# A latent attention layer and a six-layer local transformer on one core: shifted rows by two whole-tile transposes and ten small transfers, weight preparations placed one by one, another order of the pieces

## The chip, the cores and the metric

One core of a Trainium2 chip runs the whole program. Its engines are TensorE (PE; its weight loads are listed apart as PEld), VectorE (DVE), ScalarE (ACT), GpSimd (POOL) and SyncE (SP, which here only starts transfers). Each runs its own list of instructions in order and waits on semaphores for the others. The metric is the device time of one launch in microseconds (us); lower is better.

## The reference

The input is 2 batches of 1024 positions of 128 channels, float32. It is normalised; then the sum of three things is returned: the input, a causal attention with 8 heads over latent keys and values, and a transformer of 6 layers with local attention. Cut to the part that the change touches:

```python
def shift_tokens(t):                     # the upper 64 channels come from the position before
    a, s = jnp.split(t, 2, -1)
    s = jnp.pad(s, ((0, 0), (1, 0), (0, 0)))[:, :-1]
    return jnp.concatenate([a, s], -1)
def attn_layer(x, Wqkv, qs, ksc, Wo):    # 16 heads of 64, windows of 32 that also see the window before
    q, k, v = split(x @ Wqkv)
    q, k = rotate(l2norm(q) * qs), rotate(l2norm(k) * ksc)
    return local_attention(q, k, v) @ Wo
def ffn_layer(x, g, bln, W1, b1, W2, b2):
    xn = (x - mean) / sqrt(var + 1e-05) * g + bln
    a, gate = split(xn @ W1 + b1)
    return a * gelu(gate) @ W2 + b2
for i in range(6):
    x = attn_layer(shift_tokens(x), ...) + x
    x = ffn_layer(shift_tokens(x), ...) + x
```

## The kernel before

The first fifth of the time is the latent attention, which the change leaves as it is. The rest is one loop, unrolled, over steps `G`. A tile is 128 positions; a layer has 16 tiles (8 of each batch) and six layers have 96. Step `G` does a piece of work for tile `G`, another for tile `G-1` and so on, so the stages of several tiles are in flight at once. Each engine's order is the order of the calls in its own `for G in range(STEPS)` block, written by hand; a call does nothing where its tile or chunk does not exist. `chunk_at(G, lag)` names a chunk of the feed-forward part (four tiles, 512 positions) in every fourth step.

What a tile goes through, with the PE function first: `project_keys` (matmuls from `xsH`, `xsL`, `qkH`, `qkL` into PSUM banks 0 and 1; ACT squares them, DVE multiplies by the cosine and sine tables, POOL adds and scales), `transpose_keys` (ACT `copy_keys`), the same for queries, `mask_scores` and `scores`, then maxima, subtraction, exponentials, denominators and scaling, `transpose_probs` (ACT `copy_probs`). `weigh_lower` and `weigh_upper` multiply the probabilities with the shifted input itself, since the value and output matrices have been multiplied into `M` beforehand (`products`, once a layer); ACT copies both halves (`copy_lower`, `copy_upper`), and `fold_lower` and `fold_upper` apply `M`. DVE adds the residual (`attended`), PE transposes for the layer norm (`ln_rows`, `ln_columns`). The feed-forward part is `up_gate` and `up_value` in three pieces `j` each, `down`, and DVE's `residual`, which writes the next layer's input `X`.

For the weighing, `weigh_*` needs each window of 32 positions together with the window before it, 64 rows in all, with positions on the partitions, twice (partitions 0 to 63 and 64 to 127), as `xw`. PE function `windows(k)` makes it straight from `X`: 4 windows, 2 copies and 2 halves of the channels, so 16 small matmuls with the identity into banks 4 and 5, and ACT's `copy_windows` moves the 128x512 result to `xw`.

Banks: 0 and 1 hold projections, 2 and 3 transposes and products, 4 and 5 scores and weighed sums, 6 and 7 the feed-forward pieces; 6 also the layer norm's columns, 7 the folded result. `claim(bank)` waits until its last contents have been read.

At the turn of a layer: ACT's `upper_weights` rounds the raw key and query weights (inside `square_keys` and `square_queries`) and POOL subtracts; PE's `products` runs twice after `fold_upper`, with ACT's `copy_products`; `shifts` makes the new bias terms with 12 passes of one column, DVE adds them (`biases`), and in the same DVE function waits for ACT's `upper_w1` to subtract the lower part of W1. SP loads the weights of the next layer in one run, as soon as each buffer is free; `W2` has one buffer.

Of the kernel before, what the change touches and what calls it, by code (L numbers as in the profile page):

```python
# [23 lines left out]
P = 128  # L24
B, T, D = 2, 1024, 128
NT = T // P
TILES = B * NT
# [30 lines left out]
STEPS = DEPTH * TILES + 12  # L58


RING = 2


M_BANK, XW, DN_BANK = 7, 4, 7
# [31 lines left out]
def build(nc, x, wqT, wkdT, wvd, wku, wvuT, wo, wqk, wvo, w1, w2, par, sca, cst_d, tab_d, out):  # L96
    ctx = ExitStack()
    with ctx:
# [21 lines left out]
        W2 = sb("W2", [P, 3, D])  # L120
# [32 lines left out]

        arena = sb("arena", [P, 17664])
# [6 lines left out]
        xw = arena[:, 11520:12032].rearrange("p (w c) -> p w c", w=NW)  # L161
# [47 lines left out]
        for n in ("k_mm q_mm kT_mm qT_mm s_mm pt_mm xw_mm z_mm o_mm lnT_mm lnB_mm g_mm0 g_mm1 g_mm2 a_mm0 a_mm1 a_mm2 f_mm M_mm b1_mm fin_mm "  # L209
                  "k_sq q_sq kT_cp qT_cp s_exp pt_cp xw_cp z_cp ln_cp xn_cp xn_H y_sq y_ln y_exp gl0 gl1 gl2 xs_H wk_H wq_H w1_H M_cp cst_cp "  # L210
# [4 lines left out]
        c_in, qk_in, wvo_in, w1_in, w2_in, sca_in, tab_in = (  # L215
            sem(n) for n in ("c_in", "qk_in", "wvo_in", "w1_in", "w2_in", "sca_in", "tab_in"))
# [77 lines left out]
        def _(sp):  # L294
# [25 lines left out]
            def load_w2(l):  # L320
                sp.dma_start(W2[:, :, :], w2[l]).then_inc(w2_in, 16)

# [6 lines left out]
            load_w2(0)  # L329
            load_par(0)  # L330
# [4 lines left out]
            for l in range(DEPTH):  # L335
                if l + 1 < DEPTH:

                    sp.wait_ge(s["tab"], 8 * l + 8)
                    load_scales(l + 1)
# [4 lines left out]
                    load_wvo(l + 1)  # L344
                    sp.wait_ge(s["w1_L"], l + 1)
                    sp.wait_ge(s["b1_mm"], l + 1)
                    load_w1(l + 1)

                    sp.wait_ge(s["f_mm"], NC * (l + 1))
                    load_w2(l + 1)  # L350
                    sp.wait_ge(s["x_new"], NC * (l + 1))
                    if l + 2 < DEPTH:
                        load_par(l + 2)
# [7 lines left out]
        def _(pool):  # L361
            credit(pool, "pool")
            pool.memset(X[:, :, 0:XO], 0.0).then_inc(s["zeroed"], 1)
            pool.memset(X1[:, :, 0:1], 0.0).then_inc(s["zeroed"], 1)
            pool.memset(xsH[:, :, 0:1].bitcast(F32), 0.0).then_inc(s["zeroed"], 1)
# [146 lines left out]
            for G in range(STEPS):  # L512
                lower_columns(G - 7)
                scale_queries(G - 2)
                next_key_weights(G - 1)
                rotate_keys(G - 1)
                scale_probs(G - 3)
                shifted_lower(chunk_at(G, 15))
                refine(G - 1)
# [990 lines left out]
```

## Time and profile before

| | us |
|---|---|
| median of 3 runs (2095.35 to 2100.75) | 2095.5 |
| the profiled execution's own time | 2100.06 |
| its span, first to last instruction | 2098.2 |
| PE busy | 1924.6 (92%) |
| DVE busy | 1560.9 (74%) |
| POOL busy | 1324.6 (63%) |
| ACT busy | 1290.3 (61%) |

Spans and positions below are in us from the start of the profiled execution; the loop of steps begins near 400. A busy share is that of one engine alone, so that several can be high at once. An engine's idle time matters only where nothing else would have kept the following work waiting.

### The profile page before, as it was taken

The numbers are of one execution on the slowest core, as the hardware profiler recorded it, in microseconds if no ns is written. First come the engines' busy times: TensorE is split into PE (matmuls) and PEld (weight loads), VectorE is DVE, ScalarE is ACT, GpSimd is POOL, SyncE is SP. The second block draws the span as 40 slices with busy tenths as digits, with TensorE's granted clock in tenths as the row PEclk, the third lists the DMA queues.
The fourth block names the chain that finished last, engine by engine and source line by source line (L and its number), as shares of the span: only waits on it lengthen the run. The fifth ranks groups of instructions, "written<-read, shape, count | busy, mean of one in ns | idle before, by whom it ended". The sixth has DMA issues, their size and how long they took to land. (4 is left out here: it accounts for less than half of the span.)

```text
span 2098.2 us, 65778 instructions
## 1 busy us (share of the span) xinstructions
PE 1924.6 (92%) x27244; PEld 1523.1 (73%) x27244; DVE 1560.9 (74%) x2684; ACT 1290.3 (61%) x2082; POOL 1324.6 (63%) x1145
## 2 busy tenths in 40 slices
PE   6888886699999999999999999999999999999996
PEld 4665665577777777777777777777777877787774
DVE  4766865777887778877777877788776878787773
ACT  5666765356566656665656666657665666566654
POOL 2332343677786667776667866588666777676760
PEclk9999998899999999999999999999998999999999
DMA  3000001000000010000010000100000100000000
GB/s 99 2 0 0 0 1 57 15 3 2 2 2 2 2 55 2 2 3 2 2 55 2 2 2 2 55 3 2 2 2 6 52 2 2 2 3 6 2 7 16
DMA packets 12434, 25.12 MB, mean 12 GB/s; under 512 B 1856, under 2 KB 9728, under 8 KB 10496
## 3 DMA queue, kind: packets, MB, share of 16 engines
q1 hardware_dynamic: 12160, 21.16, 2.9%
q8 instruction: 209, 3.42, 0.7%
q14 instruction: 65, 0.53, 0.1%
HBM read 20.11 MB, written 1.05 MB: 10 GB/s over the span
## 5 line engine op out<-in xcount | busy, mean ns | idle before, releaser
L1061 PE MATMUL banks<-arena 128*128 128x128 f32 (+4 forms) x6052 | 672.8, 311 | 60.0 <-ACT arena L689 16.8
L1061 PEld LDWEIGHTS banks<-arena 128*128 128x128 f32 (+3 forms) x6052 | 558.5, 176 | 169.8 <-issue 70.6
L902 DVE TENSOR_TENSOR arena<-banks,tabs 128x1024 f32<-128x1024 f32 x192 | 235.2, 1225 | 133.6 <-ACT arena L646 125.0
L449 POOL TENSOR_TENSOR arena<-arena 128x1024 f32<-128x1024 f32 x96 | 230.6, 2402 | 66.0 <-DVE arena L907 65.8
L479 POOL TENSOR_TENSOR small<-small 128x33 f32<-128x33 f32 x100 | 24.6, 246 | 350.2 <-ACT small L736 350.2
L675 ACT ACTIVATE arena<-banks 128x1024 f32<-128x1024 f32 x96 | 98.7, 1028 | 238.2 <-PE banks L1218 238.2
L444 POOL TENSOR_TENSOR prob<-prob,small 128x1024 f32<-128x1024 f32 x96 | 182.7, 1903 | 82.9 <-DVE small L942 82.9
L907 DVE TENSOR_TENSOR arena<-banks,tabs 128x1024 f32<-128x1024 f32 x192 | 233.3, 1215 | 0.2 <-issue 0.2
L454 POOL TENSOR_TENSOR arena<-arena 128x1024 f32<-128x1024 f32 x96 | 228.7, 2382 | 4.0 <-DVE arena L907 4.0
L1218 PEld LDWEIGHTS banks<-cst,arena 128*128 128x128 f32 x1536 | 182.1, 142 | 28.9 <-issue 2.9
L1218 PE MATMUL banks<-cst,arena 128*128 128x128 f32 x1536 | 201.3, 275 | 1.0 <-ACT arena L675 1.0
L1061 PE MATMUL banks<-qkH,xsH 128*128 128x512 f32 x384 | 175.9, 458 | 18.9 <-DVE arena L907 18.4
L485 POOL TENSOR_TENSOR arena<-arena,small 128x1024 f32<-128x1024 f32 x96 | 182.7, 1903 | 7.6
L491 POOL TENSOR_TENSOR arena<-arena,small 128x1024 f32<-128x1024 f32 x96 | 183.0, 1906 | 0.7
L934 DVE TENSOR_REDUCE small<-arena 128x16 f32<-128x1024 f32 x96 | 116.4, 1213 | 66.5 <-ACT arena L654 66.5
L372 POOL TENSOR_TENSOR gqs<-arena,cst 128x128 fp32r<-128x128 f32 x112 | 45.7, 408 | 187.1 <-PE banks L1061 157.3
L1270 PE MATMUL banks<-arena 64*32 64x64 f32 x12288 | 144.6, 225 | 20.4 <-issue 15.8
L695 ACT ACTIVATE arena<-banks 128x1024 f32<-128x1024 f32 x96 | 98.6, 1027 | 102.8 <-PE banks L1061 102.8
L1061 PE MATMUL banks<-qkH,xsL 128*128 128x512 f32 x384 | 156.0, 406 | 0.0
L1061 PE MATMUL banks<-qkL,xsH 128*128 128x512 f32 x384 | 155.3, 405 | 0.0
L1270 PEld LDWEIGHTS banks<-arena 64*32 64x32 f32 x12288 | 128.1, 105 | 34.1 <-issue 25.4
L973 DVE TENSOR_REDUCE small<-banks 128x16 f32<-128x1024 f32 x96 | 117.4, 1222 | 38.1 <-PE banks L1270 38.1
(132 smaller groups left out, 3993.1 us busy)
## 6 DMA issues: line engine op xcount, KB each, us to landing
qkraw<-in_wqk_dram SPq DMA_DIRECT2D x6, 1024.0 KB, 5.5
arena<-in_wvo_dram SPq DMA_DIRECT2D x6, 1024.0 KB, 7.1
W<-in_w_dram SPq DMA_DIRECT2D x6, 341.0 KB, 8.6
W<-in_w_dram SPq DMA_DIRECT2D x6, 192.0 KB, 2.3
res<-in_x_dram SPq DMA_DIRECT2D x4, 256.0 KB, 4.2
tabc<-in_tab_dram SPq DMA_DIRECT2D x1, 1024.0 KB, 6.2
out_dram<-res SPq DMA_DIRECT2D x4, 256.0 KB, 2.3
sca_s<-in_sca_dram SPq DMA_DIRECT2D x6, 128.0 KB, 3.4
```

Source lines behind the costliest of these rows:

```text
L444: pool.tensor_tensor(p, p, over(den[:, :], 64), ALU.mult).then_inc(s["p_nrm"], 1)
L449: pool.tensor_tensor(kc, kc, ks, ALU.add).then_inc(s["k_add"], 1)
L454: pool.tensor_tensor(qc, qc, qs, ALU.add).then_inc(s["q_add"], 1)
L485: pool.tensor_tensor(heads(kc), heads(kc), over(rs[:, 4, 0:LH], LD), ALU.mult).then_inc(s["k_nrm"], 1)
L491: pool.tensor_tensor(heads(qc), heads(qc), over(rs[:, 4, LH:2 * LH], LD), ALU.mult).then_inc(s["q_nrm"], 1)
L902: dve.tensor_tensor(heads(c), heads(two(0)), table(k % NT, kind), ALU.mult).then_inc(s[done], 1)
L907: dve.tensor_tensor(w.rearrange("p (h z k) -> p h z k", h=LH, z=2), swapped(two(0)), table2(k % NT, kind + 1), ALU.mult).then_inc(s[done], 1)
L934: dve.reduce_sum(rin[:, LH:2 * LH], heads(sqq), AXX).then_inc(s["q_ss"], 1)
L973: dve.reduce_max(nmax[:, :], two(4).rearrange("p (h k) -> p h k", h=LH), AXX).then_inc(s["s_max"], 1)
L1061: return pe.matmul(o, l, r, start=start, stop=stop)
L1218: ins = pe.transpose(bk(2 + k // 4)[:, P * (k % 4):P * (k % 4 + 1)], src[:, P * k:P * (k + 1)], ident)
L1270: ins = pe.matmul(bk(4 + o)[WIN * w:WIN * (w + 1), 64 * j:64 * (j + 1)], qT[r, j, WIN * w:WIN * (w + 1)], kT[r, j, WIN * w:WIN * w + 64], ...
```

## The change

The 16 small matmuls of `windows` become two whole-tile transposes (`input_rows`, in the form `ln_rows` has) into banks 6 and 7, at the head of a step after `project_keys`. ACT copies 128x128 of them to `xr`, which holds the rows of two tiles. SP then builds `xw` from `xr` with ten transfers within SBUF, of 32x128 or 64x128 elements; `xw` has two buffers, in a tensor of its own. `weigh_lower` waits for the transfers.

The preparations of the weights become calls of their own at chosen places: the rounding of key and query weights, the two halves of `products` and their copies, the rounding of W1, its subtraction (out of `biases`). `shifts` moves behind `down`. SP's loads are each tied to a tile of the layer, and `W2` has two buffers. The pieces within a step stand in another order on every engine, and on POOL `next_table` stands between `refine` and `scale_keys`.

```diff
-        W2 = sb("W2", [P, 3, D])
+        W2 = sb("W2", [P, 2, 3, D])
-        xw = arena[:, 11520:12032].rearrange("p (w c) -> p w c", w=NW)
+        xw = xwr[:, 0:1024].rearrange("p (i w c) -> p i w c", i=2, w=NW)
+        xr = xwr[:, 1024:1280].rearrange("p (i c) -> p i c", i=2)
...
+            for k in range(LAST_TILE + 1):                      # SP
+                l, n = divmod(k, TILES)
+                sp.wait_ge(s["xT_cp"], k + 1)
+                if k > 1:
+                    sp.wait_ge(s["z_mm"], 2 * k - 2)
+                now, was = xr[:, k % 2, :], xr[:, (k + 1) % 2, :]
+                for o in range(2):
+                    c0 = 64 * o
+                    sp.dma_start(xw[c0:c0 + WIN, k % 2, 0, :], was[96:P, :]).then_inc(xd_in, 16)
+                    sp.dma_start(xw[c0 + WIN:c0 + 64, k % 2, 0, :], now[0:WIN, :]).then_inc(xd_in, 16)
+                    for w in range(1, NW):
+                        sp.dma_start(xw[c0:c0 + 64, k % 2, w, :], now[WIN * (w - 1):WIN * (w + 1), :]).then_inc(xd_in, 16)
+                if n == 2 and l + 1 < DEPTH:
...
+                    load_qk(l + 1)
+                if n == 5 and l + 1 < DEPTH:
...
+                    load_wvo(l + 1)
...
-            def copy_windows(k):                                # ACT
...
+            def copy_input_rows(k):
+                if is_tile(k):
+                    act.wait_ge(s["xT_mm"], k + 1)
+                    if k > 0:
+                        act.wait_ge(xd_in, XD * k)
+                    act.activation(xr[:, k % 2, :].rearrange("p (z c) -> p z c", z=2),
+                                   two(XT_BANK).rearrange("p (z c) -> p z c", z=2)[:, :, XT_COL:XT_COL + 64], ACT.Copy)                       .then_inc(s["xT_cp"], 1)
...
-            def windows(k):                                     # PE
...
-                    claim(XW, XW + 1)
-                    for w in range(NW):
-                        for o in range(2):
-                            for z in range(2):
...
+            def input_rows(k):
 
                 if is_tile(k):
                     b, i = tile_at(k)
+                    after(pe, "x_new", k // 4 - NC + 1)
+                    claim(XT_BANK, XT_BANK + 1)
+                    for z in range(2):
+                        r = slice(64 * z, 64 * z + 64)
+                        c0 = XO + P * i - z
+                        ins = pe.transpose(bk(XT_BANK + z)[:, XT_COL:XT_COL + 64], X[r, b, c0:c0 + P], ident[r, 64 * z:64 * z + 64])
+                    ins.then_inc(s["xT_mm"], 1)
+                    freed[XT_BANK] = freed[XT_BANK + 1] = ("xT_cp", k + 1)
...
             def weigh_lower(k):
                 if is_tile(k):
                     pe.wait_ge(s["pt_cp"], k + 1)
-                    pe.wait_ge(s["xw_cp"], k + 1)
+                    pe.wait_ge(xd_in, XD * (k + 1))
...
             for G in range(STEPS):                              # PE
-                ln_rows(G - 4)
                 project_keys(G)
+                input_rows(G - 2)
                 transpose_keys(G - 1)
                 weigh_lower(G - 3)
-                up_value(chunk_at(G, 10), 1)
-                up_value(chunk_at(G, 10), 0)
                 up_gate(chunk_at(G, 9), 0)
-                next_shifts(chunk_at(G, 12))
-                up_value(chunk_at(G, 11), 2)
+                up_value(chunk_at(G, 10), 0)
+                next_products_lower(G - 4)
                 up_gate(chunk_at(G, 9), 1)
+                up_value(chunk_at(G, 11), 2)
+                up_value(chunk_at(G, 10), 1)
                 down(chunk_at(G, 12))
                 weigh_upper(G - 3)
+                next_shifts(chunk_at(G, 12))
+                next_products_upper(G - 4)
                 project_queries(G)
                 transpose_queries(G - 1)
-                windows(G - 2)
                 up_gate(chunk_at(G, 9), 2)
...
                 transpose_probs(G - 2)
-                last_rows(chunk_at(G, 14))
+                ln_rows(G - 3)
+                last_rows(chunk_at(G, 13))
```

On DVE, `normalise_rows` now stands ahead of `cosine_keys` and `moments` behind `gated`, and the W1 subtraction stands last in its step, a step earlier than `biases`.

The order of PE in an ordinary step of a layer, before, from the query transposes to the end of the step (L1061 is the helper of all plain matmuls; `cst,X 64x64` is `windows`, `arena 128x128` the fold, L1356 `ln_rows`):

```order
L1218 MATMUL banks<-cst,arena 128x128 x8
L1061 MATMUL banks<-cst,X 64x64 x16
L1061 MATMUL banks<-arena 128x128 x8
L1364 MATMUL banks<-cst,lnx 128x128
L1259 MATMUL banks<-bfc 128x512 x2
L1061 MATMUL banks<-arena 128x128 x8
L1270 MATMUL banks<-arena 32x64 x64
L1218 MATMUL banks<-cst,prob 128x128 x8
L1356 MATMUL banks<-cst,X 128x64 x2
```

The same engine now, from the end of the key projection to the second half of the weighing (L1324 is `input_rows`, L1258 the key transposes, `arena,xwr` the weighing):

```order
L1101 MATMUL banks<-qkH,xsL 128x512
L1324 MATMUL banks<-cst,X 128x64 x2
L1258 MATMUL banks<-cst,arena 128x128 x8
L1101 MATMUL banks<-arena,xwr 128x256 x4
L1101 MATMUL banks<-xnH,W1H 85x512
L1101 MATMUL banks<-xnH,W1L 85x512
L1101 MATMUL banks<-xnL,W1H 85x512
L1101 MATMUL banks<-arena,xwr 128x256 x4
```

The 16 matmuls between query transposes and fold are gone, and 2 stand between key projection and key transposes.

PE at the turn of a layer, before (`parv,W 128x1` is `shifts`, `arena,W` is `down`, `arena 128x256` the weighing):

```order
L1061 MATMUL banks<-arena 128x256 x4
L1061 MATMUL banks<-parv,W 128x1 x2
L1061 MATMUL banks<-parv,W 85x1
L1061 MATMUL banks<-parv,W 128x1 x2
L1061 MATMUL banks<-parv,W 85x1
L1061 MATMUL banks<-arena,W 128x512 x3
L1061 MATMUL banks<-arena 128x256 x4
```

and now:

```order
L1101 MATMUL banks<-arena,xwr 128x256 x4
L1101 MATMUL banks<-arena,W 128x512 x3
L1101 MATMUL banks<-arena,xwr 128x256 x4
L1101 MATMUL banks<-parv,W 128x1 x2
L1101 MATMUL banks<-parv,W 85x1
L1101 MATMUL banks<-parv,W 128x1 x2
L1101 MATMUL banks<-parv,W 85x1
L1101 MATMUL banks<-qkH,xsH 128x512
```

`shifts` went from ahead of `down` to behind the second half of the weighing, ahead of the query projection.

ACT in the step of a layer's last tile, before (L646 squares the keys, L636 rounds weights, L662 is `copy_keys`, L689 `copy_lower`, L695 `copy_upper`):

```order
L646 ACTIVATE arena<-banks 128x1024
L636 ACTIVATE qkH<-qkraw 128x1024
L662 ACTIVATE arena<-banks 128x8x128
L689 ACTIVATE arena<-banks 128x2x512
L711 ACTIVATE prob<-prob 128x1024
L695 ACTIVATE arena<-banks 128x2x512
```

and now (L668 squares the keys, L710 is `copy_input_rows`, L690 `copy_keys`, L717 `copy_lower`, L723 `copy_upper`, L658 rounds weights, L679 squares the queries, L697 is `copy_queries_T`):

```order
L668 ACTIVATE arena<-banks 128x1024
L710 ACTIVATE xwr<-banks 128x128
L690 ACTIVATE arena<-banks 128x8x128
L717 ACTIVATE arena<-banks 128x2x512
L741 ACTIVATE prob<-prob 128x1024
L723 ACTIVATE arena<-banks 128x2x512
L658 ACTIVATE qkH<-qkraw 128x1024
L679 ACTIVATE arena<-banks 128x1024
L697 ACTIVATE arena<-banks 128x1024
L658 ACTIVATE qkH<-qkraw 128x1024
```

The rounding left the place between squares and key copy; the 128x128 copy stands there in every step.

## Rows read from the trace of the kernel before

**Rows 1.** Windows: us; busy us (instructions) per engine; granted clock; DMA share; GB/s.
```profile
1080.00:1340.00 260.00, 250.92 (x3845) 199.68 (x3843) 203.26 (x296) 164.11 (x239) 188.69 (x140) 0.99 0.01 3
```
**Rows 2.** Timeline, PE, a step with one feed-forward piece: start, us, line, work, [idle before].
```profile
1100.34 0.28 PE L1356 MATMUL banks<-cst,X 64*128 64x64 f32 x2
1100.54 0.49 PE L1061 MATMUL banks<-qkH,xsH 128*128 128x512 f32 x1
...
1102.05 1.04 PE L1218 MATMUL banks<-cst,arena 128*128 128x128 f32 x8
...
1105.27 1.13 PE L1061 MATMUL banks<-arena 64*128 64x256 f32 x8 [0.27 <-ACT arena L689]
...
1108.82 0.69 PE L1061 MATMUL banks<-cst,X 64*64 64x64 f32 x32
1109.44 2.05 PE L1061 MATMUL banks<-arena 128*128 128x128 f32 x16
...
1116.39 0.50 PE L1061 MATMUL banks<-qkH,xsH 128*128 128x512 f32 x1
```
**Rows 3.** Groups by form: busy us, mean ns, idle before, releasers.
```profile
L681 ACT ACTIVATE arena<-banks 128x512 f32<-128x512 f32 x96 | 57.5, 599 | 34.5 <-PE banks L1061 34.5
L717 ACT ACTIVATE lns<-banks 128x128 f32<-128x128 f32 x96 | 25.9, 270 | 2.7 <-PE banks L1356 2.7
```
**Rows 4.** Timeline, ACT, the same step.
```profile
1102.24 1.03 ACT L646 ACTIVATE arena<-banks 128x1024 f32<-128x1024 f32 x1 [0.61 <-PE banks L1061]
1103.16 1.02 ACT L662 ACTIVATE arena<-banks 128x1024 f32<-128x1024 f32 x1
1104.19 1.03 ACT L689 ACTIVATE arena<-banks 128x1024 f32<-128x1024 f32 x1
```
**Rows 5.** Waits of PE between 560 and 2030: total us, times, longest.
```profile
PE banks L1270 <- issue: 15.8, 10, 2.3
...
PE banks L1061 <- ACT arena L700: 6.1, 5, 1.2
PE banks L1270 <- ACT arena L669: 3.3, 21, 0.2
```
**Rows 6.** Timeline, PE, `shifts` and `down` at the turn of a layer.
```profile
1047.54 1.35 PE L1061 MATMUL banks<-parv,W 128*128 128x1 f32 x12
1050.25 4.51 PE L1061 MATMUL banks<-arena,W 128*128 128x512 f32 x6 [1.36 <-DVE b1p L1003]
1054.69 1.13 PE L1061 MATMUL banks<-arena 64*128 64x256 f32 x8
...
1059.42 1.80 PE L1061 MATMUL banks<-arena 128*128 128x128 f32 x14 [0.51 <-DVE X L1025]
```
**Rows 7.** Timeline, PE, `down` in the middle of a layer.
```profile
1119.93 2.85 PE L1061 MATMUL banks<-arena,W 128*128 128x512 f32 x6
```
**Rows 8.** Windows, as in Rows 1, over the slow `down`.
```profile
1050.00:1054.00 4.00, 3.75 (x6) 1.50 (x6) 0.11 (x2) 0.00 (x0) 1.63 (x1) 0.63 0.00 0
```
**Rows 9.** Timeline, PE: the weighing in a layer's last tile; the second `products`.
```profile
890.39 1.13 PE L1061 MATMUL banks<-arena 64*128 64x256 f32 x8 [1.09 <-ACT arena L689]
...
952.21 1.16 PE L1061 MATMUL banks<-arena 64*128 64x128 f32 x16 [1.22 <-ACT arena L700]
```
**Rows 10.** Timeline, POOL, key scaling of the step in Rows 2.
```profile
1113.78 1.91 POOL L485 TENSOR_TENSOR arena<-arena,small 128x1024 f32<-128x1024 f32 x1
```
**Rows 11.** Timeline, SP: two small transfers started.
```profile
1059.31 0.33 SPq L324 DMA_DIRECT2D parv<-in_par_dram  x1
1059.68 0.43 SPq L312 DMA_DIRECT2D sca_s<-in_sca_dram  x1
```
**Rows 12.** Issues between 1054 and 1075: KB, us to landing.
```profile
sca_s<-in_sca_dram SPq DMA_DIRECT2D x1, 128.0 KB, 3.1
parv<-in_par_dram SPq DMA_DIRECT2D x1, 4.5 KB, 3.2
```
**Rows 13.** Groups by form, POOL: the rotary table's scaling.
```profile
L380 POOL TENSOR_TENSOR tabs<-tabc,sca_s 128x256 f32<-128x256 f32 x48 | 35.1, 731 | 0.0
```

More of the change, by code:

```diff
@@ L214, in build @@
             s[n] = sem(n)
[L215 to L216 removed]
+        c_in, qk_in, wvo_in, w1_in, sca_in, tab_in = (
+            sem(n) for n in ("c_in", "qk_in", "wvo_in", "w1_in", "sca_in", "tab_in"))
+        xd_in = sem("xd_in")
+        w2_in = [sem("w2_in0"), sem("w2_in1")]
         par_in = [sem("par_in0"), sem("par_in1")]
@@ L334, in _ @@
             load_wvo(0)
[L335 to L339, printed above, removed]
+            sp.wait_ge(s["zeroed"], CR + 6)
+            for k in range(LAST_TILE + 1):
[11 more added lines that the diff above has]
+                if n == 2 and l + 1 < DEPTH:
                     sp.wait_ge(s["wk_L"], l + 1)
@@ L342, in _ @@
                     load_qk(l + 1)
+                if n == 5 and l + 1 < DEPTH:
                     sp.wait_ge(s["M_mm"], 2 * l + 2)
                     load_wvo(l + 1)
+                if n == 7 and l + 1 < DEPTH:
+                    sp.wait_ge(s["tab"], 8 * l + 8)
+                    load_scales(l + 1)
+                if n == 10 and 0 < l and l + 1 < DEPTH:
+                    sp.wait_ge(s["f_mm"], NC * l)
+                    load_w2(l + 1)
+                if n == 12 and l > 0 and l + 1 < DEPTH:
+                    sp.wait_ge(s["x_new"], NC * l)
+                    load_par(l + 1)
+                if n == 13 and l + 1 < DEPTH:
                     sp.wait_ge(s["w1_L"], l + 1)
@@ L512, in _ @@
             for G in range(STEPS):
[L513 to L519, printed above, removed]
-                scale_keys(G - 1)
                 lookback(G - 1)
-                next_query_weights(G - 1)
                 rotate_queries(G - 1)
-                next_table(G - 1)
+                scale_queries(G - 1)
+                rotate_keys(G)
+                scale_probs(G - 2)
+                shifted_lower(chunk_at(G, 14))
+                next_key_weights(G)
+                refine(G)
+                next_table(G - 2)
+                scale_keys(G)
+                lower_columns(G - 5)
+                next_query_weights(G)
         @block.scalar
@@ L1019, in next_biases, with next_w1_lower @@
                     biases(c // NC + 1)
+            def next_w1_lower(c):
+                if c is not None and c % NC == NC - 1 and c < DEPTH * NC - 1:
+                    w1_lower(c // NC + 1)
             def residual(c):
@@ L1342, in fold_upper, with next_products_lower, next_products_upper @@
                     freed[M_BANK] = ("x1", k + 1)
-                    if k % TILES == TILES - 1 and k < LAST_TILE:
-                        products(k // TILES + 1, 0)
-                        products(k // TILES + 1, 1)
+            def next_products_lower(k):
+                if is_tile(k) and k % TILES == TILES - 1 and k < LAST_TILE:
+                    products(k // TILES + 1, 0)
+            def next_products_upper(k):
+                if is_tile(k) and k % TILES == TILES - 1 and k < LAST_TILE:
+                    products(k // TILES + 1, 1)
             def ln_rows(k):
```

133 lines of the change are left out of this document (67 added, 66 removed).

## The prediction

> **What bounds the kernel now.** I read the busy times by stretch first, then one step on PE's timeline, then the same step on ACT, last the list of what PE waits for. In a stretch in the middle of the loop PE is busy 250.92 of 260 us, DVE 203.26, POOL 188.69, ACT 164.11 [rows 1]. So 96.5% of the time is PE's, and the others have 22% or more to spare: an edit counts if it takes work or a wait off PE, and costs if it makes PE wait. The timeline confirms it: one step runs from 1100.54 to 1116.39, 15.85 us, back to back but for 0.27 us [rows 2]. A busy PE is not by itself PE-bound, as starts overlap; therefore I take each price from the start of a piece to the start of the next.
>
> What is left of PE's idle time is small and of few kinds [rows 5]: 15.8 us in ten places within `scores` that the profile lays to no engine, 6.1 us at the second `products` (five times), 3.3 us before `scores` in steps with gelu. The 0.27 us in [rows 2] is a wait for ACT's `copy_lower`, which stands in an unbroken ACT chain after the key projection: squares, key copy, lower copy at 1102.24, 1103.16, 1104.19 [rows 4].
>
> **The windows.** `windows` runs from 1108.82 to the fold's start at 1109.44, 0.62 us. Two transposes of the form that comes in take from 1100.34 to 1100.54, 0.20 us [rows 2]. So PE does 0.42 us less in each of 96 steps. ACT copies 128x128 in 0.27 us instead of 128x512 in 0.60 us [rows 3], but the copy now stands inside the ACT chain of [rows 4], and `copy_lower` ends 0.27 us later after the key projection. PE reaches `weigh_upper` 0.20 us later (its transposes). Where a step has two feed-forward pieces or `down` there, PE needs at least 1.6 us longer than in [rows 2] and the copy is ready; there the gain is the full 0.42. In the value step of every fourth tile, and in the few steps before the first chunk, PE waits for `copy_lower` already; there the gain is 0.62 - 0.27 = 0.35 us. With 72 and 24 such steps: 72 x 0.42 + 24 x 0.35 = 38.6 us.
>
> **The transfers.** After a tile's copy SP starts ten transfers. A start of such size takes 0.33 and 0.43 us [rows 11]; ten take some 4.3 us, and the last lands about 3.2 us later [rows 12]: 7.5 us in all. The copy ends 1.5 us after the key projection; the weighing that needs it comes one step later, 16.6 us after the same point, so 15.1 us are there for 7.5. Price taken: 0. Bounds: nothing (hidden), and the wait of the rival below. Behind SP's waits stand only the weight loads, whose conditions (a layer's earlier pieces) have long held at their tiles; none of them blocks the ten transfers. Two loads issued 0.37 us apart landed 0.27 us apart, at 1062.5 and 1062.8, though each takes over 3 us [rows 11, 12]: they overlap.
>
> The Trainium skill, DMA: Bandwidth & Descriptors, under Anatomy of one DMA, puts about 2.0 us of fixed cost on each transfer of the software path, most of it waiting for the write receipt, and under Bandwidth calls transfers below 64 KB descriptor-dominated. If that cost were paid ten times in a row, an estimate from the page gives 20 us per tile, more than a step; the landings above speak for overlap, and by them the page's figure is paid once.
>
> **The order within a step.** In steps with gelu, one piece of gelu and the table load now stand ahead of `copy_upper`, the query copy ahead of the column copies. That should end the 0.16 us before `scores` (3.3 us in 21 steps [rows 5]) and may add a wait for bank 7 of about 0.2 us, 24 times, 4.8 us. I take +1.5 us; bounds -3 and +10, the latter if 0.4 us is lost in each. `next_table` ahead of `scale_keys` makes the keys 0.73 us later [rows 13] in ten steps of a layer. The scaling ends at 1115.69 [rows 10], PE's key transposes come 15.85 us after 1102.05, at 1117.90: 2.2 us of slack. Price 0. The DVE moves (`normalise_rows` ahead, `moments` back) fill the time in which DVE waits for the squares: 0.
>
> **The turn of a layer, five times.** (1) `shifts` and `down`: from 1047.54 to 1054.69 are 7.15 us where `down` alone takes 2.85 [rows 6, 7], and 0.51 us of waiting follow: 4.8 us extra. Of it 1.35 is `shifts`, 1.36 a wait for DVE's bias add, and about 1.6 is `down` at a clock granted at 0.63 on average over 4 us [rows 8], that is partly at the lower level, 1.2 GHz, after a stretch of one-column passes and idling. Now `shifts` follows the weighing, and nobody needs bank 7 before the fold, about 2.5 us later; DVE's add comes in time. I keep 1.35 and drop 3.45: 17.3 us for five. The bounds: 9 us if the clock still falls (1.6 us each stay), 17.3 if not; one-column passes remain, but wait and `down` behind them are gone, and waits of 1.2 us elsewhere [rows 9] leave no such slow group. (2) The second `products` waits 1.22 us for ACT [rows 9]; now they are apart, with the copy between. I leave 0.3 us for the first (it now follows close on the key copy): 0.9 x 5 = 4.5 us. (3) In the last tile's step PE waits 1.09 us instead of 0.27 for `copy_lower` [rows 9], since the weight rounding stands in ACT's chain. It leaves it, but POOL now does the key subtraction before `refine` and the table, and the query subtraction before `lookback`; by my count of POOL's list the next key copy is late by some 0.4 us. Gain 0.4 x 5 = 2, bounds -5 and +4. Together 23.8 us.
>
> **What is not touched.** The ten unexplained waits in `scores` [rows 5] fall at the same two tiles of each layer. The Trainium skill, Runtime: NRT & Kernel Launch, under Instruction fetch mechanics, says that an engine's instructions come in blocks of 16 KiB, 256 of them, mostly hidden. `scores` is the densest burst: 64 matmul calls recorded as 128, with as many weight loads, in 1.4 us. What the page gives for the sum is the same, no change, but it would let the places move. With fewer instructions per step the pattern shifts; I take 0, between -16 (all gone) and +20 us (twice as many).
>
> **The sum.** 38.6 - 1.5 + 23.8 = 61 us. Against the profiled execution's own time, 2100.06 (its span is 2098.2), that is 2039; this execution stood 4.6 us above the median, so against the median 2095.5 it is 2034.5. I forecast 2034.
>
> **The rivals.**
> - *The gain returns in part as another wait* (ACT's or POOL's chain, which now has to come round every 15.4 us). For it: 24 steps already touch `copy_lower`, and both chains got longer at their critical place. Against it: POOL's 2.2 us and the 22% of DVE. If 0.3 us comes back in every step, 96 x 0.3 = 29 us: about 2064.
> - *The transfers are late*, slower than before. The mechanism: ten transfers for one tile through one queue, one after the other; ACT's next copy waits for them and PE's `weigh_lower` too. It decides from 1.5 us per transfer (15.1 us through 10). At 3.1 us each, as a lone one takes [rows 12], a tile needs 31 us instead of 16.6 on average: 96 x 14.6 = 1400 us more, about 3440. By the page's 2.0 us it would be an estimate of 2360. Against it: the overlapping landings.
> - *The unexplained waits multiply*, slower than before. Each longest one is 2.3 us [rows 5], and slow clock after it costs as in (1) another 1.6. From 16 more of them the 61 us are used up; one in every fourth step would be 24 x 3.9 = 94, so 2095.5 - 61 + 94 = 2128. For it: they come with dense bursts and nothing here thins `scores`. Against it: a burst of 16 matmuls leaves every step.
> - *The change does not do what it says*: the windows were hidden. Then only the turns count: about 2072. Against it: PE starts the fold only behind them, back to back.
>
> **Chances.** Forecast with its own range 2012 to 2052: 0.68. Part returned, 2064: 0.17. Hidden windows, 2072: 0.04. Late transfers 0.04, more waits 0.05, no change 0.02. A difference under 0.3% (6 us) can't be told from none. So faster 0.89, same 0.03, slower 0.08. The range of 8 in 10 is 2010 to 2070: the low end with the unexplained waits and half the small ones gone (-16, -8), the high end past the partial return.
>
> **What would show it.** In the profile after: the group of 64x64 matmuls gone and the small transposes at 192 more; steps in mid-layer at about 15.5 us where [rows 2] has 15.85 and 0.42 less in the others; `shifts` followed at once by a projection at full clock; no wait of PE on transfers. Wrong would be: a wait on a transfer before the weighing, steps shorter by less than 0.3 us, a half-clock stretch after `shifts`, or more time in waits without an owner within `scores`.

## The result and the profile after

| | before | after |
|---|---|---|
| median of timed runs, us | 2098.1 (4 runs, 2095.4 to 2104.1) | 2046.1 (4 runs, 2040.4 to 2053.1) |
| ratio, 95% interval | | 0.975 (0.971 to 0.979) |
| profiled execution, span, us | 2098.2 | 2043.4 |
| PE busy, DVE busy, us | 1924.6, 1560.9 | 1873.4, 1656.8 |

The change takes off 52 us. The forecast was 61, and 2034 for the time; the measured 2046 is 12 us above that and lies in the forecast's own range (2012 to 2052). The reasons are less good than the sum.

The page of the kernel after, part 1:

```profile
PE 1873.4 (92%) x24364; PEld 1471.0 (72%) x24364; DVE 1656.8 (81%) x2684; ACT 1264.6 (62%) x2082; POOL 1331.1 (65%) x1146
```

PE's busy time falls by 51.2 us. DVE's rises by 95.9 us, though DVE got hardly any work. The same stretch as in [rows 1]:

```profile
1080.00:1340.00 260.00, 252.23 (x3588) 199.69 (x3587) 231.14 (x310) 166.73 (x249) 196.78 (x146) 1.00 0.11 28
```

DVE (the third value) had 22% to spare in [rows 1], and has 11% now. What PE waits for, 560 to 1860 us, before and then after (total us, times, longest). [Rows 5] has three of these rows, taken up to 2030 us (its last one has 3.0 us up to 1860, the other two are the same); here are the others over 2 us (two smaller ones without an owner have 1.3 and 0.9):

```profile
PE banks L1061 <- ACT arena L689: 9.0, 18, 1.1
PE banks L1061 <- DVE b1p L1003: 5.5, 4, 1.4
```

```profile
PE banks L1101 <- DVE arena L939: 22.8, 33, 0.9
PE banks L1310 <- issue: 5.2, 3, 1.9
PE banks L1101 <- DVE X L1063: 4.8, 4, 1.2
PE banks L1101 <- ACT arena L717: 3.7, 14, 0.3
PE banks L1399 <- DVE X L981: 3.4, 11, 0.4
PE banks L1258 <- issue: 3.2, 3, 1.4
```

Before, all PE waits of this stretch sum to 43.3 us; after, to 43.1. The old ones fell (`copy_lower`, L689, now L717, from 9.0 to 3.7; the bias add and the second `products` are gone), and one that had been 0.2 us, `project_keys` waiting for DVE's `sine_queries` (L939), took their place, with two smaller ones on DVE (the residual L1063, `attended` L981). The shares without an owner went from 15.8 + 1.3 + 0.9 to 5.2 + 3.2.

Where DVE's time went, by line, before and then after (busy us, mean ns):

```profile
L988 DVE TENSOR_SCALAR lnx<-lns,small 128x128 f32<-128x128 f32 x73 | 32.9, 451 | 0.0
L968 DVE TENSOR_TENSOR small<-small 128x33 f32<-128x33 f32 x74 | 14.3, 194 | 7.7
```

```profile
L1020 DVE TENSOR_SCALAR lnx<-lns,small 128x128 f32<-128x128 f32 x76 | 102.7, 1351 | 0.0
L1000 DVE TENSOR_TENSOR small<-small 128x33 f32<-128x33 f32 x77 | 45.4, 589 | 8.0
L966 DVE TENSOR_REDUCE small<-arena 128x16 f32<-128x1024 f32 x77 | 93.7, 1216 | 67.0 <-ACT arena L679 66.6
```

`normalise_rows` (L988, now L1020) is the same instruction on the same data and takes three times as long. The second product in `seeds` (L968, now L1000) does too. The large reduction doesn't (1213 ns before at L934). The timeline of POOL, DVE and PE in one step with a value piece tells why (start, duration):

```profile
1404.69 2.38 POOL L476 TENSOR_TENSOR arena<-arena 128x1024 f32<-128x1024 f32 x1
1404.97 2.18 DVE L1020 TENSOR_SCALAR lnx<-lns,small 128x128 f32<-128x128 f32 x1
...
1415.37 1.29 POOL L412 TENSOR_TENSOR xsL<-X,xsH 64x512 fp32r<-64x512 f32 x1
1415.58 1.14 DVE L997 TENSOR_TENSOR small<-small 128x33 f32<-128x33 f32 x1
1416.74 1.28 POOL L415 TENSOR_TENSOR xsL<-X,xsH 64x512 fp32r<-64x512 f32 x1
1416.82 1.25 DVE L1000 TENSOR_TENSOR small<-small 128x33 f32<-128x33 f32 x1
...
1419.33 1.21 DVE L939 TENSOR_TENSOR arena<-banks,tabs 128x1024 f32<-128x1024 f32 x1
...
1420.68 0.47 PE L1101 MATMUL banks<-qkH,xsH 128*128 128x512 f32 x1 [0.90 <-DVE arena L939]
```

POOL's `rotate_queries` (L476) ends at 1404.69 + 2.38 = 1407.07, `normalise_rows` at 1407.15. POOL's two halves of `shifted_lower` end at 1416.66 and 1418.02, the two `seeds` products at 1416.72 and 1418.07. Each time DVE's instruction ends just behind POOL's that ran when it began: its duration is a wait. The whole trace says the same. Of the 96 `normalise_rows`, 81 are long (over 1.25 times the shortest), and each of them ends 0.08 to 0.09 us behind the POOL instruction that ran when it began; of the 100 second `seeds` products 25 are long, and they end 0.04 to 0.06 us behind POOL's. None that began with POOL idle is long, in either. Everything behind it is late (`cosine_keys`, later `sine_queries`), and PE stands 0.90 us before the next key projection.

The Trainium skill, SBUF — State Buffer, under Who interferes with whom, says that a `tensor_scalar` out of and into SBUF may take the port pair that GpSimd uses too and whoever comes second is blocked for the whole instruction, a `tensor_tensor` with two SBUF inputs contends likewise, and a reduction never does. The three rows above agree (451 to 1351 ns, 194 to 589, 1213 to 1216). The forecast did not weigh this rule, and it speaks against the move.

The turn of a layer, on PE, which answers to [rows 6], and the window behind it, which answers to [rows 8] (granted clock third from the end):

```profile
1033.24 2.85 PE L1101 MATMUL banks<-arena,W 128*128 128x512 f32 x6
...
1038.31 1.33 PE L1101 MATMUL banks<-parv,W 128*128 128x1 f32 x12 [1.16 <-DVE X L1063]
...
1041.13 1.91 PE L1258 MATMUL banks<-cst,arena 128*128 128x128 f32 x8
```

```profile
1040.00:1044.00 4.00, 4.00 (x19) 3.62 (x19) 1.82 (x6) 1.95 (x2) 1.56 (x1) 0.60 0.02 4
```

`down` runs at full clock in 2.85 us, as forecast. But now `shifts` itself waits 1.16 us for the residual (L1063), and the clock falls behind it: eight key transposes take 1.91 us where 1.07 is usual. The wait stands at four of the five turns, the slow clock behind it at three. On DVE, the residual (L1063) stands behind a long `normalise_rows`:

```profile
1032.20 1.92 DVE L1020 TENSOR_SCALAR lnx<-lns,small 128x128 f32<-128x128 f32 x1
...
1037.43 0.74 DVE L1063 SCALAR_TENSOR_TENSOR X<-banks,parv,X 128x512 f32<-128x512 f32 x1
```

The mid-layer steps, from the mask matmul of one value step to that four steps later:

```profile
1602.10 0.59 PE L1299 MATMUL banks<-bfc 128*128 128x512 bf16 x2
1667.89 0.59 PE L1299 MATMUL banks<-bfc 128*128 128x512 bf16 x2
```

That is 65.79 us, where the kernel before needs 66.81 (1376.41 to 1443.22). A gain of 1.0 us for four steps, where four times the 0.42 would be 1.7. It is not spread evenly. From the start of one key projection to the next, the last four steps of the fourth layer take 17.41, 17.32, 16.24 and 16.67 us before and 16.96, 16.54, 17.06 and 17.04 after: the first two got 0.5 and 0.8 us shorter, the last two, at whose end PE waits for `sine_queries`, 0.8 and 0.4 us longer.

The transfers: SP's first and last starts for one tile, and then the page's list (KB each, us to landing), which answer to [rows 11, 12]:

```profile
1406.55 0.54 SPq L351 DMA_DIRECT2D xwr<-xwr  x1
...
1411.03 2.69 SPq L354 DMA_DIRECT2D xwr<-xwr  x3
```

```profile
xwr<-xwr SPq DMA_DIRECT2D x576, 32.0 KB, 1.9
...
xwr<-xwr SPq DMA_DIRECT2D x384, 16.0 KB, 1.8
```

The starts lie some 0.6 us apart. From a tile's first start to its last landing it takes 7.6 to 9.2 us (median of the 96 tiles 8.1; 8.7 for the tile shown); 7.5 was forecast. The weighing begins 5.5 us or more behind the last landing, and no wait of PE names a transfer.

### The profile page after: what moved, and what is told of

Read it like the earlier page. It is cut to its first block, busy times and chain, and to the rows that moved or that the text cites. A ratio compares the mean times of both kernels' runs of the same rounds, so it can differ in the third digit from the quotient of the medians.

```text
span 2043.4 us, 61163 instructions
## 1 busy us (share of the span) xinstructions
PE 1873.4 (92%) x24364; PEld 1471.0 (72%) x24364; DVE 1656.8 (81%) x2684; ACT 1264.6 (62%) x2082; POOL 1331.1 (65%) x1146
## 4 chain that ended last, share of the span: by engine, by line
PE 62%; DVE 23%; issue 9%; ACT 4%; POOL 1%; DMA 1%; DVEq 0%; SPq 0%; ACTq 0%; POOLq 0%
PE banks L1101 44%; PE banks L1258 9%; DVE arena L939 4%; PE banks L1310 4%; DVE arena L934 3%; DVE small L885 2%; PE banks L1185 2%; DVE small L1005 2%; DVE small L966 2%; PE banks L1299 1%; DVE lnx L1020 1%; DVE small L961 1%; DVE arena L1048 1%; DVE small L997 1%; DVE small L972 1%
## 5 line engine op out<-in xcount | busy, mean ns | idle before, releaser
L1101 PE MATMUL banks<-arena 128*128 128x128 f32 (+3 forms) x4516 | 450.9, 280 | 32.3 <-DMA arena<-in_wqT_dram 10.1
L1101 PEld LDWEIGHTS banks<-arena 128*128 128x128 f32 (+3 forms) x4516 | 426.5, 173 | 69.8 <-issue 19.1
L934 DVE TENSOR_TENSOR arena<-banks,tabs 128x1024 f32<-128x1024 f32 x192 | 234.3, 1220 | 62.4 <-PE banks L1258 52.7
L939 DVE TENSOR_TENSOR arena<-banks,tabs 128x1024 f32<-128x1024 f32 x192 | 232.9, 1213 | 0.2 <-issue 0.2
L476 POOL TENSOR_TENSOR arena<-arena 128x1024 f32<-128x1024 f32 x96 | 228.5, 2380 | 0.0
L1101 PE MATMUL banks<-arena,xwr 64*128 64x256 f32 x1536 | 217.8, 402 | 11.3 <-ACT arena L717 11.3
L1258 PE MATMUL banks<-cst,arena 128*128 128x128 f32 x1536 | 209.5, 280 | 0.1
L1258 PEld LDWEIGHTS banks<-cst,arena 128*128 128x128 f32 x1536 | 176.7, 143 | 21.0 <-issue 1.7
L1101 PEld LDWEIGHTS banks<-arena,xwr 64*128 64x128 f32 x1536 | 132.2, 186 | 81.7 <-issue 47.8
L966 DVE TENSOR_REDUCE small<-arena 128x16 f32<-128x1024 f32 x96 | 116.8, 1216 | 83.3 <-ACT arena L679 82.9
L668 ACT ACTIVATE arena<-banks 128x1024 f32<-128x1024 f32 x96 | 98.5, 1026 | 95.5 <-PE banks L1101 95.5
```

Of the source, the lines that this page charges most:

```text
L476: pool.tensor_tensor(qc, qc, qs, ALU.add).then_inc(s["q_add"], 1)
L934: dve.tensor_tensor(heads(c), heads(two(0)), table(k % NT, kind), ALU.mult).then_inc(s[done], 1)
L939: dve.tensor_tensor(w.rearrange("p (h z k) -> p h z k", h=LH, z=2), swapped(two(0)), table2(k % NT, kind + 1), ALU.mult).then_inc(s[done], 1)
L966: dve.reduce_sum(rin[:, LH:2 * LH], heads(sqq), AXX).then_inc(s["q_ss"], 1)
L1101: return pe.matmul(o, l, r, start=start, stop=stop)
L1258: ins = pe.transpose(bk(2 + k // 4)[:, P * (k % 4):P * (k % 4 + 1)], src[:, P * k:P * (k + 1)], ident)
```

## The experiments

The theory: the windows' 36 us of work did go, but DVE fell behind since it waits for POOL, and PE waits for DVE. The rivals: the slow form of `normalise_rows` has another cause; the windows were hidden; ACT or POOL set the end. Medians, and ratios against the kernel before on the same chip (e1 to e4, e5 to e8 and e9 to e12 had a chip each):

| | kernel | us | ratio (95%) |
|---|---|---|---|
| | after | 2046.1 | 0.975 (0.971 to 0.979) |
| e1 | after, normalise_rows back | 2033.6 | 0.967 (0.965 to 0.969) |
| e2 | after, other walk | 2045.5 | 0.973 (0.972 to 0.975) |
| e3 | after, shifts later | 2032.0 | 0.968 (0.966 to 0.971) |
| e4 | after, windows by matmul | 2056.3 | 0.979 (0.976 to 0.981) |
| e5 | before, normalise_rows ahead | 2094.3 | 0.998 (0.997 to 1.000) |
| e6 | after, POOL reordered | 2033.7 | 0.969 (0.966 to 0.971) |
| e7 | e1 + e3 + e6 | 2019.8 | 0.963 (0.960 to 0.965) |
| e8 | e7, windows by matmul | 2044.1 | 0.974 (0.972 to 0.976) |
| e9 | e7, POOL once more | 2019.2 | 0.962 (0.960 to 0.964) |
| e10 | before, shifts later | 2081.9 | 0.991 (0.989 to 0.992) |
| e11 | after, constants | 2046.9 (one run) | |
| e12 | after, constants, other walk | 2042.3 (one run) | |

e2 has the time of after and ran beside e1, e3 and e4. Against it they are 11.9 and 13.5 us faster and 10.8 us slower, so the differences to after given below do not come from the chip.

**e1: normalise_rows behind the key rotation.**

```diff
-                normalise_rows(G - 5)
                 cosine_keys(G)
                 sine_keys(G)
+                normalise_rows(G - 5)
```

> The changed kernel with one call of DVE moved: normalise_rows stands behind sine_keys again, where it stood before the change. Theory (the wait moved to DVE): its 128x128 subtraction and scaling, SBUF to SBUF, now meets POOL's 2.4 us addition and waits for it (mean 1351 ns between 560 and 1860 where before it had 451); that makes DVE late and PE waits at project_keys for sine_queries (39.6 us in 39 waits). So: mean of the operation below 600 ns, DVE busy 80 to 90 us less, PE's wait for the sine at most 12 us, time 20 to 30 us below the changed kernel's 2046, about 2021. Rival (DVE is late because of the pieces of gelu and the layer norm's moments that moved, the operation is long but would be hidden): mean falls, time within 6 us of 2046.

```profile
L1020 DVE TENSOR_SCALAR lnx<-lns,small 128x128 f32<-128x128 f32 x77 | 33.5, 435 | 0.0
```

```profile
PE banks L1101 <- DVE arena L939: 21.4, 24, 0.9
```

The instruction takes 435 ns again, and 12.5 us come back, less than expected. The wait for `sine_queries` stays nearly whole (21.4 of 22.8 us), so `normalise_rows` is not its cause: it stands behind the value steps, where `seeds` meets `shifted_lower` as in the timeline above, and behind a layer's last step, where it meets POOL's subtraction for the key weights. What comes back is at the turn:

```profile
1033.37 0.34 DVE L1020 TENSOR_SCALAR lnx<-lns,small 128x128 f32<-128x128 f32 x1
...
1034.84 0.75 DVE L1063 SCALAR_TENSOR_TENSOR X<-banks,parv,X 128x512 f32<-128x512 f32 x1
```

The residual begins 2.88 us behind the start of `down` (1031.96 here), in after 4.19 (1033.24). The wait of `shifts` is gone at all turns (4.8 us in after) and with it the slow clock. The step with `down` at a turn, from the start of its key projection to the next one's, is shorter by 9.8 us in the sum over the five turns.

**e2: another walk over the same data.** In `normalise_rows` input and output are walked as `"p (c z) -> p z c"`, z = 2.

> The changed kernel, same order, but the operands of normalise_rows are walked in another order of elements: channel pairs apart, so that the innermost step is two elements on both sides; the same numbers come out. Theory A (the long time is a lock: in its fast form the operation takes the port that POOL uses and must wait for POOL's running instruction; the Trainium skill, SBUF - State Buffer, says so of two-port forms): without the fast form nothing waits, mean 250 to 400 ns at the same place, time 20 to 30 us below the changed kernel. Theory B (any SBUF to SBUF operation of DVE waits while POOL runs one): mean stays near 1350 ns and the time near 2046.

The mean is 1330 ns, the time that of after: this walk waits as long. Theory B fits, and so does theory A if this walk does not leave the fast form (see e12).

**e3: shifts behind the query projection.**

```diff
-                next_shifts(chunk_at(G, 12))
                 next_products_upper(G - 4)
                 project_queries(G)
+                next_shifts(chunk_at(G, 12))
```

> The changed kernel with shifts one place later, behind project_queries. Theory (shifts waits 1.2 us for DVE to read the result of down, and the clock falls after that wait together with the one-column passes): wait gone, no stretch at the lower clock after three or more of the five turns, 5 x 1.2 + 4 x 1.5 = 10 to 12 us less, near 2035. Rival (the one-column passes alone make the clock fall, and DVE then waits for them in the bias add and passes the wait on): 0 to 6 us less.

```profile
1031.52 1.25 PE L1101 MATMUL banks<-parv,W 128*128 128x1 f32 x12
1032.63 1.07 PE L1258 MATMUL banks<-cst,arena 128*128 128x128 f32 x8
```

Minus 14.1 us: the wait is gone at all turns and with it the slow clock (1.07 us for the transposes, granted clock 1.00 from 1031 to 1035). The five steps with `down` at a turn are 10.0 us shorter together, much as in e1: both edits mend the same wait, one by an earlier residual and one by later `shifts`.

**e4: the windows by matmul in the changed kernel.** `windows` with its 16 matmuls and ACT's 128x512 copy return, behind `transpose_queries` and `square_queries`; two buffers and all else stay.

```diff
-                input_rows(G - 2)
...
+                windows(G - 2)
```

> The changed kernel with xw made by the 16 matmuls and the 128x512 copy of before (into the two-buffer xw), at their former places; no transfers within SBUF, everything else as changed. Theory (PE's work sets the time, the transfers are hidden): 0.35 to 0.42 us more in each of 96 steps, 34 to 40 us more than the changed kernel, about 2083. Rival (DVE's lateness sets many steps now, so PE's saving is partly idle time): 15 to 25 us more, about 2066.

```profile
PE banks L1092 <- DVE arena L930: 10.7, 21, 0.6
PE banks L1092 <- DVE X L1054: 5.0, 5, 1.1
PE banks L1092 <- ACT arena L708: 3.6, 14, 0.3
...
PE banks L1301 <- issue: 0.3, 1, 0.3
```

(L1092 and L930 are here the matmul helper and `sine_queries`.) PE busy is 1909.5 us, 36.1 above after: the forecast's 38.6 us of work are there. The time is only 10 us longer (7 by the ratios). In the stretch PE waits 20.4 us instead of 43.1. Both numbers on record missed this. So most of the windows' gain was eaten by waits in the changed kernel. That the work on PE hides DVE's lateness is one reading of it: the wait for `sine_queries` is 10.7 us here, 22.8 in after. Another part has no owner, 0.3 us here and 8.4 in after. And the rest of the change (kernel before to e4) is worth some 45 us, twice my 22.

**e5: the DVE move alone, in the kernel before.** `normalise_rows(G - 6)` goes ahead of `cosine_keys(G - 1)`.

> The kernel before with one call of DVE moved: normalise_rows ahead of cosine_keys, as the changed kernel has it. Theory (a lock: its SBUF to SBUF form waits for POOL's running instruction): its mean rises from 431 to 1000 ns or more, DVE busy by 50 to 90 us. PE's wait at the projections for DVE's sine grows by 5 to 15 us, and the time by as much over the kernel before, 2101 (same chip) to about 2111. Rival (the long operation came with the shorter steps of the change and not with its place): mean below 600 ns, no change of time.

The mean goes from 451 to 859 ns, DVE is busy 36 us more, and the time is the same: a miss. In the kernel before nothing on PE was waiting for what became late; `shifts` stands ahead of `down` there and does not need the residual. Longer steps alone do not help: in e4, with the windows' work back, `shifts` still waits at all five turns (5.0 us). It is the move together with the new place of `shifts` that costs.

**e6: POOL's order.**

```diff
                 scale_probs(G - 2)
-                shifted_lower(chunk_at(G, 14))
-                next_key_weights(G)
                 refine(G)
-                next_table(G - 2)
+                next_key_weights(G)
                 scale_keys(G)
+                next_table(G - 2)
+                shifted_lower(chunk_at(G, 14))
                 lower_columns(G - 5)
```

> The changed kernel, POOL's order alone edited: refine first, then next_key_weights, scale_keys, next_table, and shifted_lower last of these. Theory (DVE's two seed multiplications of 128x33 wait for POOL's subtractions of 1.3 and 2.4 us: in the value steps and in a layer's last tile): the mean of the second one falls from 589 to below 350 ns, PE's wait for the sine from some 31 us between 560 and 1860 to below 20, time 8 to 18 us below the changed kernel, about 2033. Rival (keys or the next layer's input now come late instead): a new wait of PE on POOL, time within 5 us of 2046.

```profile
L1000 DVE TENSOR_TENSOR small<-small 128x33 f32<-128x33 f32 x77 | 14.9, 194 | 8.0
```

```profile
PE banks L1101 <- ACT arena L717: 13.7, 19, 1.2
```

The `seeds` product is back at 194 ns and the wait for `sine_queries` is gone, though `normalise_rows` still takes 1123 ns: POOL's place for `shifted_lower` and `next_key_weights`, both of which this edit moves, was what made it. 12.4 us are gained. The wait at the turn stays (7.0 us), and a new wait takes a part: POOL's `lookback` now stands behind `shifted_lower`, ACT's key copy waits for it, and PE for ACT's `copy_lower`:

```profile
1412.68 0.40 POOL L493 COPY arena<-arena 128x256 f32<-128x256 f32 x1
...
1413.17 1.03 ACT L690 ACTIVATE arena<-banks 128x1024 f32<-128x1024 f32 x1 [1.18 <-POOL arena L493]
1414.09 1.02 ACT L717 ACTIVATE arena<-banks 128x1024 f32<-128x1024 f32 x1
...
1415.16 1.13 PE L1101 MATMUL banks<-arena,xwr 64*128 64x256 f32 x8 [1.25 <-ACT arena L717]
```

**e7: the three together** (edits of e1, e3 and e6).

> normalise_rows back, shifts behind project_queries, and POOL's order of the run before this one, together, on the changed kernel. If the three gains are separate: 2046 - 12 - 14 - 13 = 2007. If normalise_rows and POOL's order remove the same wait: 2015 to 2022.

2019.8 us, 26.3 below after; the three single gains sum to 39.0. The time is where the expectation put it for an overlap of e1 and e6, but the overlap is that of e1 and e3, which mend the same wait at the turn: the gains of e3 and e6 alone sum to 26.5, and the five steps of the turn are 10.0 us shorter than in after, no more than with e1 or e3 alone. (e3 and e6 without e1 were not run.)

**e8: e7 with the windows by matmul**, as in e4.

> As the run before this one, but xw made by the 16 matmuls and the 128x512 copy, no transfers within SBUF. Theory (the windows' saving was hidden in the changed kernel by DVE's lateness, 10 us of 38 arrived): with DVE on time the difference to the run before this one is 30 to 40 us, about 2043. Rival (PE's saving arrives only in part for another reason, such as waits within scores without an owner that come with fewer instructions): 10 to 20 us.

24.3 us slower than e7, at 34.5 us more PE work (1899.3 against 1864.8). That lies between the two ranges expected (30 to 40, 10 to 20). Without the waits for DVE most of the windows' gain arrives; in e4 against after it was 10. The missing 10 us are waits again: in the stretch PE waits 27.2 us in e7 and 15.3 in e8, and 7.3 of the difference have no owner (11.0 against 3.7), so the expected rival has a part in it.

**e9: POOL once more.**

```diff
-                lookback(G - 1)
                 rotate_queries(G - 1)
...
                 rotate_keys(G)
+                shifted_lower(chunk_at(G, 14))
                 scale_probs(G - 2)
...
                 scale_keys(G)
+                lookback(G)
                 next_table(G - 2)
-                shifted_lower(chunk_at(G, 14))
```

> The combination of three (2020), with POOL's order edited once more: shifted_lower between rotate_keys and scale_probs, where POOL waits for the denominators anyway and DVE reads from PSUM, and lookback behind scale_keys in the same step. Theory (what is left of PE's waits there comes from ACT's key and lower copies, which wait for a late lookback: 19.4 us in all at copy_lower): the wait at copy_lower falls to 9 us, time 8 to 12 us less, about 2010. Rival (a late scaling of the probabilities takes its place): 2020 or more.

```profile
PE banks L1101 <- DVE arena L939: 4.6, 19, 0.5
...
PE banks L1101 <- ACT arena L717: 3.7, 14, 0.3
PE banks L1258 <- POOL arena L513: 2.9, 5, 0.6
```

The wait for `copy_lower` falls from 14.4 us in e7 to 3.7, and two others come up. The time is that of e7, not 10 us less: a miss. e7 and e9 are the best versions, 1.3% below after.

**e10: shifts later, in the kernel before.** `next_shifts` goes behind `weigh_upper`, `residual` ahead of `next_biases`; nothing else.

> The kernel before with shifts behind weigh_upper and, since DVE would otherwise wait for itself, residual ahead of next_biases. This is term (1) of the turn alone. By the prediction 5 x 3.45 = 17 us less, 2082 on this chip. By what the changed kernel's trace shows (shifts waits 1.2 us for DVE's residual, and the clock still falls in most turns) 5 x 1.4 = 7 us less, 2092.

```profile
1043.10 2.85 PE L1061 MATMUL banks<-arena,W 128*128 128x512 f32 x6
...
1046.94 1.36 PE L1061 MATMUL banks<-parv,W 128*128 128x1 f32 x12
1048.15 0.48 PE L1061 MATMUL banks<-qkH,xsH 128*128 128x512 f32 x1
```

19.0 us less, 17.3 was the term. No wait, no slow clock behind it (granted 1.00 from 1047 to 1051). My lower guess for this run was wrong, the term right.

**e11, e12: normalise_rows with constants**, in place of mean and factor from SBUF, in the walk of after and in that of e2. Both leave the layer norm out; they are read for this instruction alone.

> The changed kernel, normalise_rows with constants (subtract 0.5, times 0.5) in place of the two per-row numbers from SBUF; the layer norm is not computed. Its operands stay contiguous. If the lock comes with the fast form of a contiguous float32 operation: still near 1300 ns. If it comes with the two per-row operands, a second reader of SBUF: 200 to 300 ns.

> As the run before this one, constants, and the strided walk of the second experiment. If either the fast form or the per-row operands alone are enough for the lock: 200 to 400 ns here, while the other three cases stay long. If any operation from SBUF to SBUF waits: near 1300 ns here too.

```profile
L1020 DVE TENSOR_SCALAR lnx<-lns x96: 217/1232/2194, 444.0 to 2026.4; 128x128 f32<-128x128 f32 x96
```

The shortest, median and longest duration (ns) of e11; e12 has 218, 1239 and 2194. Undisturbed it is shorter than with mean and factor from SBUF (217 against 336), but it waits as before, in both walks. So neither the two operands from SBUF nor the contiguous walk is needed for the wait. The Trainium skill, VectorE: DVE Perf Modes, under Mode 2×_2P, asks of an operation with one source tensor only that both tensors are in SBUF and the outermost non-unit dimension is even; the walk with z = 2 outermost meets that, so by this rule e2 and e12 could not have avoided the wait, and they agree. A walk that breaks this condition was not tried.

## Why the prediction was right and where it failed

The forecast time came out, partly by luck: an error of some 30 us (the windows) and one of 23 (all else) stood against one another.

- **The windows, 38.6 us.** The work was sized right (36.1 on PE, after against e4; 34.5, e7 against e8), but as time only 7 to 11 us arrived in the changed kernel and 24 in the mended one. The step that failed is the overlap: "the others have 22% or more to spare", and the price of nothing for the orders of DVE and POOL. The prediction asked whether DVE had time, not beside what on POOL its instructions would stand. Two places cost. In the value steps and a layer's last step `seeds` runs into POOL's `shifted_lower` and key subtraction, and PE waited 22.8 us for `sine_queries`; e6 removes that and is 12 us faster. At the turn the moved `normalise_rows` makes the residual late; e1 removes that and is 12 us faster. So "fill the time in which DVE waits for the squares: 0" was wrong too: 70 us more of DVE time in the stretch, harmless in most steps and in the kernel before (e5), but not where `shifts` needs the residual.
- **The transfers, 0.** Right: 7.6 to 9.2 us for ten, overlapping, and never waited for. The serial rival (3440) and that by the 2.0 us each of the Trainium skill, DMA: Bandwidth & Descriptors, Anatomy of one DMA (2360), are out. One took 1.7 to 3.5 us here from start to landing, so the trace has a cost of that size for each, but ten side by side.
- **The turn, 17.3 us.** The old stall was sized right: e10 alone gives 19.0, 17.3 of it in the five steps of the turn. In the changed kernel a part came back at the new place, a wait of 1.2 us for the residual at four turns and slow clock at three of them; the turn's steps lose 10.0 us by it, which e3 and e1 each get back. The text had "wait and `down` behind them are gone" and looked only at `down`; that `shifts` needs DVE's residual, itself made late by the first point, it passed over. "What would show it wrong" named this: a half-clock stretch after `shifts`.
- **The other small terms** (products 4.5, weights 2, order -1.5). The wait at `products` went (6.1 us in five), that for `copy_lower` went from 9.0 to 3.7, that of 3.0 before `scores` vanished. They were taken too low by some 9 us. Before to e4, all but the windows, is 45 us where my terms give 22; the larger part of the missing 23 is the next point.
- **The waits without an owner, 0.** Priced between -16 and +20. They went from 18.0 us in the stretch to 8.4 in after, 0.3 in e4, 3.7 in e8, and up to 20.4 in e10. Of the 22.9 us by which PE waits less in e4 than in the kernel before, they are 17.7. The price left out what follows them. At three of the four waits of 2.2 to 2.3 us the clock fell in the kernel before, with no one-column pass near:

```profile
1009.00:1013.00 4.00, 4.00 (x34) 3.07 (x34) 2.45 (x2) 1.19 (x2) 3.60 (x4) 0.64 0.02 4
```

  The step in which such a wait stands took 20.7, 20.0, 19.8 and 21.0 us in four layers, and 17.3 in the last one, where it has none: 12 us for waits of 9.0. In the whole stretch the clock record has 30.7 us at the lower level before, 10.2 in after and 3.4 in e4. The waits go with the program (e1, e2, e3, e11 and e12, close to after, have 7 to 12 us, e5 and e10, close to the kernel before, 17 and 20) and not with any edit I could name, so a forecast of nothing was a guess, and the gain from them is luck. What they are stays open; nothing tried tells it.
- **The sum.** 61 against 52: the windows brought 7 to 11 in place of 38.6, all else some 45 in place of 22. The total was closer than its parts. By steps, 49 of the 55 us between the two profiled executions come from three steps of each of the last five layers: the one with the products (19.7), the one with the long wait without an owner (16.1), the turn (12.9). Of the rivals, "the gain returns in part as another wait" (2064) was right in kind, and it named ACT's or POOL's chain and against it "the 22% of DVE", where DVE was the engine. Two rivals are summed a little off (2073 for hidden windows, not 2072; 14.4 us for each tile of late transfers, not 14.6), which changes nothing.

## What to carry to other kernels

Before a moved VectorE instruction is priced at nothing, look at what GpSimd runs at its new place: if the moved one reads and writes SBUF, compare the shortest and median duration of that line; a gap is a wait, not work. Work taken off the bounding engine arrives only as far as the engines behind it come round in the shorter step: name who sets each of them free and add up their waits too. When an instruction moves behind another engine's result, as `shifts` behind `down`, ask what else now has to be ready there. Compare the lengths of single steps, not only the totals: a gain in most steps and a loss in every fourth can't be told apart in a sum. Put one-column passes where nothing is waited for ahead of them.

## What the runs showed of the hardware

- `normalise_rows` and the `seeds` products, VectorE instructions between SBUF operands, when they were long ended 0.04 to 0.09 us after the GpSimd instruction that ran when they began (81 of 96 and 25 of 100 in after): 217 to 337 ns of work were recorded as up to 2194 ns. Reductions (1213 to 1216 ns) and products with a PSUM input (1225 to 1219 ns at `cosine`) kept their time.
- Ten small transfers within SBUF from one queue, started 0.6 us apart, landed 1.8 to 1.9 us after their starts in the median (1.7 to 3.5), so side by side.
- The 12 one-column passes alone don't bring the clock down: it stayed at 1.00 behind them at every turn of e3 and e10. With a wait of 1.2 us ahead of them the granted clock was at its lower level (1.2 GHz) soon behind them in three of four cases in after, 0.60 on average over 4 us; with 1.0 to 1.1 us ahead of them in e4 in one of five. Three of the four waits of 2.2 to 2.3 us in the kernel before had a slow stretch at their end without such passes (0.54 to 0.64 over 4 us), the fourth had none.
